# Letting the first expert blocks start before the last scatters, with a third of the expert weights loaded in the last main beat

## The reference

```python
x = x + attention(layernorm(x))               # causal, rotary positions
h = layernorm(x).reshape(4096, 256)
topv, topi = top_k(h @ gate_w.T, 8)           # 8 of 64 experts for each token
rw = softmax(topv)
gu = einsum('nh,eih->nei', h, gu_w)           # 64 gate and 64 up values for each expert
out_e = (silu(gate) * up * W) @ dp_w          # W holds rw at the chosen experts, 0 elsewhere
out = sum over experts of out_e + sigmoid(h @ sg) * shared_ffn(h)
x = x + out
```

## Time and profile before

| what | value |
|---|---|
| runs | 1210.23, 1207.71, 1210.20 us |
| median | 1210.2 us |
| span of the profiled execution | 1382.2 us |
| instructions | 23533 |
| TensorE matmul busy | 1080.5 us (78%) |
| DVE busy | 703.8 us (51%) |
| ACT busy | 647.6 us (47%) |
| POOL busy | 722.5 us (52%) |

### The profile page before, as it was taken

One profiled execution on the slowest core, in us unless ns is written; L12 is line 12 of the kernel. 1 busy time (PEld: TensorE's weight loads), 2 busy tenths in 40 slices (PEclk: granted clock), 3 DMA queues, 4 the chain that ended last, 5 costly groups with the idle time before them and its releaser, 6 DMA issues.

```text
span 1382.2 us, 23533 instructions
## 1 busy us (share of the span) xinstructions
PE 1080.5 (78%) x7305; PEld 833.1 (60%) x7305; DVE 703.8 (51%) x2197; ACT 647.6 (47%) x1586; POOL 722.5 (52%) x953
## 2 busy tenths in 40 slices
PE   3799998888888888889765058887888878787875
PEld 1566666565565656566534047777777767676763
DVE  3476766666666666656525411121245544444447
ACT  2465656555555555655331024444445444444441
POOL 3111225657466564564566735655565565655552
PEclk9699999999999989989877569999999999998996
DMA  2586877212122121122228855555767777776536
GB/s 82 174 288 221 275 256 237 101 48 95 51 84 93 53 90 51 59 102 61 84 93 289 269 172 161 172 169 154 238 233 251 268 268 248 259 243 238 170 138 212
DMA packets 142824, 233.18 MB, mean 169 GB/s; under 512 B 17303, under 2 KB 119910, under 8 KB 137840
## 3 DMA queue, kind: packets, MB, share of 16 engines
q1 hardware_dynamic: 67936, 101.06, 22.7%
q0 software_dynamic: 27600, 69.28, 14.1%
q10 hardware_dynamic: 47168, 61.35, 13.5%
HBM read 107.32 MB, written 132.53 MB: 174 GB/s over the span
## 4 chain that ended last, share of the span: by engine, by line
PE 46%; DVE 16%; another core or an unknown queue 14%; issue 13%; ACT 8%; POOL 1%; DMA 1%; ACTq 0%; SPq 0%; DVEq 0%; POOLq 0%
PE psB L1412 6%; DVE nmax L868 6%; PE psD L1429 5%; PE psv L607 4%; PE ps L511 4%; PE psA L1402 4%; PE ps L558 3%; PE ps L518 3%; PE psp L490 3%; PE psp L504 3%; PE psC L1420 3%; ACT xT L1297 2%; ACT y L1313 2%; PE psq L634 2%
## 5 line engine op out<-in xcount | busy, mean ns | idle before, releaser
L1497 POOL DMA_INDIRECT res_d<-y,dst_i x319 | 320.9, 1006 | 231.9 <-ACT y L1313 117.8
L463 POOL DMA_INDIRECT rows_d<-pay,slot_i x256 | 256.5, 1002 | 75.4 <-issue 73.4
L868 DVE TENSOR_REDUCE nmax<-ps 128x1 f32<-128x512 f32 (+3 forms) x448 | 225.8, 531 | 135.8 <-PE ps L518 93.5
L736 ACT ACTIVATE wgu_s<-ps 128x512 f32<-128x512 f32 x320 | 191.9, 600 | 123.4 <-PE ps L518 91.3
L1216 DVE TENSOR_TENSOR inner<-inner,psB 128x128 f32<-128x128 f32 x160 | 45.8, 286 | 316.8 <-ACT inner L1302 250.5
L1429 PE MATMUL psD<-wdp_s,innerT 128*128 x638 | 174.8, 397 | 21.1 <-ACT innerT L1306 17.6
L1412 PE MATMUL psB<-wgu_s,xT 128*128 x1276 | 179.1, 285 | 1.2 <-ACT xT L1297 0.8
L518 PE MATMUL ps<-mask,ident_b 128*128 128x256 bf16 (+1 forms) x640 | 175.4, 274 | 0.4 <-issue 0.4
L511 PE MATMUL ps<-kT,qT 96*128 96x512 f32 (+3 forms) x512 | 168.3, 391 | 8.1 <-DVE nmax L868 4.8
L558 PE MATMUL ps<-qT,kT 128*128 128x512 f32 (+3 forms) x512 | 165.8, 387 | 4.9 <-ACT wgu_s L736 4.2
L1412 PEld LDWEIGHTS psB<-wgu_s,xT 128*128 128x128 f32 x1276 | 163.9, 201 | 1.8 <-issue 1.2
(11 more groups left out here) (256 smaller groups left out, 1620.0 us busy)
## 6 DMA issues: line engine op xcount, KB each, us to landing
rows_d<-blank ACTq DMA_DIRECT2D x8, 5440.0 KB, 19.3
xg<-rows_d SPq DMA_DIRECT2D x160, 272.0 KB
yk<-res_d SPq DMA_DIRECT2D x28, 1024.0 KB
wgu_s<-wgu_in ACTq DMA_DIRECT2D x8, 1024.0 KB
x_d<-x SPq DMA_DIRECT2D x30, 192.5 KB
xs<-x_d SPq DMA_DIRECT2D x30, 192.5 KB, 2.5
res_d<-y,dst_i POOLq DMA_INDIRECT x319
wgu_s<-x_in SPq DMA_DIRECT2D x32, 128.0 KB, 2.2
```

What stands on the lines that cost most here:

```text
L463: pool.indirect_dma_start(rows_d, bass.IndirectOffsetOnAxis(ap=slot_i[par][:, t, k:k + 1], axis=0), pay[par][:, t, :], None).then_inc(s_sc ...
L736: act.activation(pexp[p % 4][:, s, :], ps2[:, (5 * p + s) % 2, :], ACT.Exp, scale=HEAD_D ** -0.5).then_inc(s_exp, 1)
L868: return dve.tensor_reduce(nmax[u][:, tile, heads[0]:heads[-1] + 1], src, AX.X, ALU.max, negate=True)
L1497: pool.indirect_dma_start(res_d, bass.IndirectOffsetOnAxis(ap=dst_i[:, j % (2 * G):j % (2 * G) + 1], axis=0), y[:, j % Y, :], None, bounds ...
```

## The change

Four things are done.

- SP's wait for the scatters is split. It waits for all of `s_scat[0]`, then, ahead of blocks 0 and 16, for `s_scat[1]` against a value read from SBUF, and ahead of block 32 for all of `s_scat[1]`. The value is computed in the route of the last batch: if some expert's open block lies below block 16 (or 32), it is the full count, otherwise the count without the last batch.
- Two of the eight gate-up parts and two of the four down parts are loaded in the last main beat, at the start of p = 3, 4, 5, 6. The zeroing of the upper partitions beside those two down parts is cut into 16 DVE memsets of 512 columns in the first four slots of p = 4 to 7 of that beat. The other two are zeroed after the attention phase, as before.
- `inner` is zeroed by DVE, not POOL; DVE's first use of `sh` waits for POOL's memset.
- For the value of `needed`, DVE has five short operations more and TensorE one matmul more in the last batch's route.

```diff
+EARLY_BLOCKS = 16
+        EARLY = 2
+        below = cst[0:EXPERTS, C_MASK1:C_MASK1 + EARLY]
+        needed = cst[0:1, C_MASK2:C_MASK2 + EARLY].bitcast(I32)
...
+                        if ending(h, par, 1):
+                            pe.wait_ge(e_open, 3)
+                            pe.matmul(psq[0:EXPERTS, 2:2 + EARLY], ones_f[0:EXPERTS, 0:EXPERTS], below,
+                                      start=True, stop=True)
...
+            EARLY_GU, LATE_GU = (6, 7), (0, 1, 2, 3, 4, 5)
+            EARLY_DOWN, LATE_DOWN = (0, 2), (1, 3)
...
+                    if now and now[0] * 2 + now[1] == BATCH - 1 and s == 0 and now[2] >= 3:
+                        act.wait_ge(s_split_ps, 4 * ALL_TILES)
+                        act.wait_ge(s_s2, (BATCH - 1) * SLOTS)
+                        if now[2] - 3 < len(EARLY_GU):
+                            load_gate_up(EARLY_GU[now[2] - 3])
+                        elif now[2] - 3 - len(EARLY_GU) < len(EARLY_DOWN):
+                            load_down(EARLY_DOWN[now[2] - 3 - len(EARLY_GU)])
...
+                    if h * 2 + par == BATCH - 1 and p >= 4 and s < 4:
+                        n, width = (p - 4) * 4 + s, EXPERTS * D // (8 * TILES)
+                        if n == 0:
+                            dve.wait_ge(s_s2, (BATCH - 1) * SLOTS)
+                        at = EARLY_DOWN[n // 8] * 8 * width + n % 8 * width
+                        last = dve.memset(wdp_s[INNER:P, at:at + width], 0.0)
+                        if n == 15:
+                            last.then_inc(e_padded, 1)
...
+                    if k == 0 and ending(h, par, 1):
+                        dve.wait_ge(s_pool, 12 * b)
+                        dve.tensor_scalar(col[:, 15:16], col[:, 0:1], col[:, 1:2], 2.0 ** 20, ALU.is_ge,
+                                          ALU.mult).then_inc(e_open, 1)
+                        dve.wait_ge(e_open, 1)
+                        dve.scalar_tensor_tensor(out=col[:, 15:16], in0=col[:, 0:1], scalar=col[:, 2:3],
+                                                 in1=col[:, 15:16], op0=ALU.add, op1=ALU.add).then_inc(e_open, 1)
+                        dve.wait_ge(e_open, 2)
+                        dve.tensor_scalar(below, cst[0:EXPERTS, C_BLK + EARLY_BLOCKS:C_BLK + EARLY * EARLY_BLOCKS + 1:
+                                                     EARLY_BLOCKS], col[:, 15:16], None, ALU.is_gt).then_inc(e_open, 1)
...
+                        if ending(h, par, 1):
+                            last_batch = 16 * TILES * TOP
+                            dve.tensor_scalar(below[0:1], psq[0:1, 2:2 + EARLY], 0.5, float(last_batch), ALU.is_gt,
+                                              ALU.mult).then_inc(e_open, 1)
+                            dve.wait_ge(e_open, 4)
+                            dve.tensor_scalar(needed, below[0:1], float(last_batch * (BATCH // 2 - 1)), None,
+                                              ALU.add).then_inc(e_needed, 1)
...
-                for par in range(2):
-                    sp.wait_ge(s_scat[par], 16 * TILES * TOP * BATCH // 2)
+                sp.wait_ge(s_scat[0], 16 * TILES * TOP * BATCH // 2)
+                sp.wait_ge(e_needed, 1)
...
+                    if j % EARLY_BLOCKS == 0 and j // EARLY_BLOCKS < EARLY:
+                        n = j // EARLY_BLOCKS
+                        scattered = sp.value_load(needed[0:1, n:n + 1], min_val=16 * TILES * TOP * (BATCH // 2 - 1),
+                                                  max_val=16 * TILES * TOP * BATCH // 2)
+                        sp.wait_ge(s_scat[1], scattered)
+                    if j == EARLY * EARLY_BLOCKS:
+                        sp.wait_ge(s_scat[1], 16 * TILES * TOP * BATCH // 2)
...
-                dve.memset(wdp_s[INNER:P, :], 0.0).then_inc(e_wdp_zero, 1)
+                for part in LATE_DOWN:
+                    last = dve.memset(wdp_s[INNER:P, part * EXPERTS * D // TILES:(part + 1) * EXPERTS * D // TILES], 0.0)
+                last.then_inc(e_padded, 1)
+                for t in range(TILES):
+                    dve.wait_ge(s_x2out[t], 16 * (2 * BATCH - 1) if t < 2 else 16)
+                dve.memset(inner[:], 0.0).then_inc(e_padded, 1)
...
+                    if tile == 0:
+                        dve.wait_ge(e_zero, 1)
...
-                act.wait_ge(e_zero, 2)
+                act.wait_ge(e_padded, 3)
...
-                pe.wait_ge(e_wdp_zero, 1)
+                pe.wait_ge(e_padded, 2)
...
-                pool.memset(inner[:], 0.0).then_inc(e_zero, 1)
```

More of the change, by code:

```diff
@@ L81, in build @@
         e_wdp = sem("down_weights_in")
-        e_wdp_zero = sem("down_weights_padded")
+        e_padded = sem("down_weights_and_inner_padded")
+        e_open, e_needed = sem("open_blocks"), sem("scatters_needed")
         waits_met = sem("waits_met")
@@ L737, in exps, with load_gate_up, load_down @@
                                    scale=HEAD_D ** -0.5).then_inc(s_exp, 1)
-                def main(now, one, two, s):
+                def load_gate_up(part):
+                    width = EXPERTS * KC * GU // (2 * TILES)
+                    cut = slice(part * width, (part + 1) * width)
+                    act.dma_start(wgu_s[:, cut], wgu[:, cut]).then_inc(e_w, 16)
+                def load_down(part):
+                    width = EXPERTS * D // TILES
+                    cut = slice(part * width, (part + 1) * width)
+                    act.dma_start(wdp_s[0:INNER, cut], wdp[:, cut]).then_inc(e_wdp, 16)
+                def main(now, one, two, s):
+                    if now and now[0] * 2 + now[1] == BATCH - 1 and s == 0 and now[2] >= 3:
[5 more added lines that the diff above has]
+                            load_down(EARLY_DOWN[now[2] - 3 - len(EARLY_GU)])
                     if now and isinstance(now[0], int):
@@ L773, in post @@
                         act.wait_ge(s_s2, BATCH * SLOTS)
[L774 to L781, removed]
+                        part = (t - 2) * 6 + k
+                        if part < len(LATE_GU):
+                            load_gate_up(LATE_GU[part])
+                        elif part - len(LATE_GU) < len(LATE_DOWN):
+                            load_down(LATE_DOWN[part - len(LATE_GU)])
                     if k == 1:
```

## The result

| what | before | after |
|---|---|---|
| median of the runs | 1209.45 us (4 runs, 1207.71 to 1210.23) | 1196.03 us (4 runs, 1193.35 to 1196.32) |
| ratio of after to before | | 0.9879, 95% interval 0.9863 to 0.9896 |

The change makes the kernel 14.6 us faster ((1 - 0.9879) x 1209.45; by the interval 12.6 to 16.6). The ratio is the recorded one with its interval and not the quotient of the two medians, which is 0.9889 and would give 13.4 us. The prediction was 15.3 us.

What follows compares the result with a forecast made beforehand. Without the unknown pieces POOL was taken as slightly slower than TensorE, the two near even later. Gain 19.6 less cost 4.3 (4 + 1.5 - 1.2) is 15.3 us: 1210.2 to 1194.9 us, range 1184 to 1206.

Steps and rivals of the forecast that it cites:

- the unknown pieces: Chain time in the first profile put down to nothing known, 14%; taken as mostly the profiler's own.
- The rival in which TensorE and ACT pace: Expert phase: TensorE's whole ten-block lead counts, 24 to 28 us less 4.3, about 1188 us; chance 0.13.
- a span near 1359: Profiled execution after the change: at 1.69 us a block, 27.9 us gained less 4.3, from 1382.2.
- step 1: SP's gate: loads may start once batch 6 lands, at 764; reading a value 1.5 us, priced at nothing.
- step 2: Weights at the handover: a third less to load late, 17.7 us earlier; TensorE starts at about 780, not 809.
- step 4: POOL at the handover: 14.1 us saved plus 3.7 of early starvation, 17.8; with TensorE's lead 21.4; middle taken, 19.6.
- step 5: The 16 memsets in the last main beat: cost 4 us, half hidden, bounds 0 and 8.8.
- The other bound, a bare 8.8: Memsets in the last main beat not hidden; as a rival, with 2 us of route, about 1203 us; chance 0.16.
- steps 6 and 7: Last batch: longer route costs 1.5 us on the path; ACT's four DMA issues leaving its post save 1.2 us.
- slower-side rival: Expert phase: TensorE's clock stays low after its pause; gain gone at some 63 us, 1235 us at 50 blocks; chance 0.04.

Runs made afterwards that it cites:

- before_again: The kernel before, unchanged, profiled once more (also written "before, again"): 1209.27 us, profiled span 1207.5 us.
- pool_slower: late_zeros with 39 memsets of 768 columns on POOL, one before every eighth block: 1213.51 us, ratio to the kernel before 1.0038.
- gate_only: The changed kernel with all twelve weight parts and all zeroing back behind the attention phase, SP's split wait kept: 1191.78 us, ratio 0.9869.
- late_zeros: The changed kernel without the 16 memsets, all 16,384 columns zeroed after the attention phase, early weights kept: 1191.6 us, ratio 0.9848.
- zeros_thrice: The changed kernel with each of the 16 memsets done three times, each waiting for the one before: 1210.33 us, ratio 1.0001.
- weights_only: The changed kernel with SP again waiting for all scatters before its first load: 1210.92 us, ratio 1.001.
- no_pool_wait: late_zeros without POOL's wait for its last rows_d scatter and its zeroing of `sh`, which DVE does at first use: 1189.88 us, ratio 0.984.
- eight_early: late_zeros with gates at blocks 4 and 8, so 8 blocks and not 32 may go ahead of the last scatters: 1197.62 us, ratio 0.9903.

## Why the prediction was right

**What paces.** The argument was that the unknown pieces of the profile are its own and that POOL paces behind the handover. before_again shows the first. The second is shown by POOL's idle time in after, by ACT's 94.8 us for room in `y`, and by pool_slower, where a delay of 23.8 us put into POOL's queue showed as 21.8. The rival in which TensorE and ACT pace falls with it. The forecast of a span near 1359 was wrong: it took over from one execution a stretching that the next one didn't have.

**The gate opens (step 1).** Shown: SP's first load is at 718.55, 5.2 us behind the end of batch 6's last scatter where 3.3 were forecast (762.24 to 764 + 1.5), and POOL has 28 of batch 7's scatters still to issue. The count of the reference's choices held.

```profile
718.55 81.56 SPq L1217 DMA_DIRECT2D xg<-rows_d  x35
```

**TensorE's start (step 2).** Forecast 15.5 us behind the first scatter of batch 7, held by the weights; measured 7.6 us (721.25 - 713.66), held by the loads: the last weight part is issued at 689.83 and lands 25.8 us later, at 715.6, before SP's first load. Wrong by 8 us, on the safe side, and worth nothing, since POOL was busy for 32 us more. For the same reason the weights part, which the step counted as 17.7 us, is worth nothing: gate_only shows it.

**POOL at the handover and behind it (step 4).** Forecast 14.1 + 3.7 = 17.8; measured 13.98 + 3.18 = 17.16. The step then went up to 19.6, halfway to the 21.4 that TensorE's lead would give if TensorE paced the later blocks. That is the part that failed: POOL has no waits behind block 95 either, after or in before, again, so the lead is worth nothing. The gain was 2.4 too high.

**The 16 memsets (step 5).** The mechanism is right (partly hidden in DVE's gaps), the size is not: forecast 4, measured 1.0. I had taken as cover only the 5.7 us ahead of the reductions that wait for TensorE, read from the stretched execution, whose row puts another 12.3 us ahead of the same reductions down to other causes. In before, again DVE waits 11.4 us for TensorE's scores in that part of the beat, and after 5.0: the cover was twice what I had read, and the memsets used 6.4 us of it. By the runs alone 4 could not be excluded (3.7 in late_zeros). The other bound, a bare 8.8, nearly comes true for each further round: 16.5/2 = 8.3 us in zeros_thrice.

**Route and ACT's issues (steps 6 and 7).** Forecast +1.5 and -1.2; measured 0 and 0 within what can be read: 86.67 us before, again, 86.95 after, and 86.66 in weights_only, from batch 6's `slot_i` to the last rows_d scatter. The step had the route of batch 7 on the path because POOL idled 2.26 us for it. In before, again POOL has no such gap: it goes from 708.93 to 710.19 in its usual step. After, batch 7's slots are ready while POOL is still in batch 6's scatters:

```profile
708.33 0.18 DVE L333 TENSOR_SCALAR slot_i<-slot_f 128x32 int32<-128x32 f32 x1
```

POOL's last scatter of batch 6 starts at 712.39, 3.9 us behind its end. So POOL's own queue sets the start of batch 7's scatters, and a longer route is hidden. The 2.26 us belonged to the stretched execution.

**The sum.** Forecast 19.6 - 4.3 = 15.3; by terms measured 17.2 - 1.0 = 16.2, the trace has 16.0, the runs 14.6. The gain was too high by 2.4 and the cost by 3.3, and they cancelled in part: that the total is so close (0.7 us from the runs) is luck, two errors in gain and cost that offset each other. Either error alone would have left the time inside the range of 1184 to 1206.

**The clock.** TensorE's idle time was the slower-side rival. It came as described: TensorE stops for 12.66 us.

```profile
763.29 2.04 PE L1498 MATMUL psD<-wdp_s,innerT 128*128 x4 [12.66 <-ACT innerT L1375]
```

It resumes at 1.2 GHz, that is at 0.50 in 755 to 765 (the windows above), shows 0.68 in 765 to 770 and 1.00 from 770, the 2.4 GHz level. Low clock thus ends less than 7 us after the restart, and ten blocks lie ready, so POOL never sees it; the rival needed 63 us. (It took 2.35 us a block at that level; half of its 4.74 is 2.37, which changes nothing.) The Trainium skill (TensorE: Matmul & The Clock Gate, HAM oscillation) describes such a swing; the trace agrees, with this one dip (1.00, 0.50, 1.00) behind the handover, and it had no price here.

## What to carry to other kernels

Ask which queue paces behind a handover and work out a gain only from the waits of that queue: here POOL's wait was worth its 14 + 3 us to the end, while a third of the weights loaded early was worth nothing, nor was it that the first blocks lay ready 24 us before POOL took them. Price an added piece against the waits of its engine in that stretch, read from an execution that is not stretched, and remember that this cover is used up: the first 16 memsets cost a tenth of their length, the next 32 four fifths. Where a profile's span is far from the time of the runs, profile the same kernel again before you read waits and gaps in it, and compare executions from a marker, not from their start.

## What the hardware showed that I had not expected

- **How late a POOL scatter lands when weights are loading.** SP's first load waits for the last scatter of batch 6 to land. It follows that scatter's end by 5.2 us after (713.35 to 718.55), and by 2.7, 4.0, 4.4 and 2.7 us in late_zeros, no_pool_wait, eight_early and pool_slower; about 1 us of each is SP's own reading of the value. In gate_only, where all twelve weight parts load late, it follows by 15.9 us (706.44 to 722.35), at a DMA share of 1.01 in 706 to 722, and that SP waits there for the scatters is in its waits (us in all, times, longest):

```profile
SPq L1202 <- DMA rows_d<-pay,slot_i: 7.4, 1, 7.4
```

  In before, again, where the weights are late as well, the landing itself comes 18.1 us behind the end of that scatter, against 14.9 in gate_only and 4.0 after. POOL went on issuing every 1.27 us all the while. The cause inside the DMA engines was not tried; here it was hidden.
- **A memset's row is shorter than the memset.** The two late memsets after, of 4096 columns:

```profile
710.16 3.47 DVE L1248 MEMSET wdp_s<- 64x4096 f32 x1 [0.91 <-DMA x_d<-oT]
714.43 3.47 DVE L1248 MEMSET wdp_s<- 64x4096 f32 x1 [0.80 <-DMA x_d<-oT]
```

  From start to start it is 4.27 us, 1.04 ns a column, against 0.85 by the row. The Trainium skill (VectorE: DVE Perf Modes, Zero memsets can be issued as uint32) has one cycle an element, 1.04 ns at the 0.96 GHz of its Specifications; by the spacing the trace agrees, by the row it doesn't. The idle time that nothing explains ahead of a memset grows with its length: 0.16 us at 512 columns, 0.80 at 4096, and 3.47 at 16,384 in before, again. (The releaser named at 0.80 is not it: the same 0.80 stands in gate_only between late memsets with no releaser.)
- **A memset on POOL among scatters costs less than its row**: 0.61 us for a row of 0.78, since the gap behind it is 0.16 us and not 0.30 and it starts before the scatter's row has quite ended.
- **One profiled execution can be stretched**: 1382.2 us of span against 1207.5 for the same kernel, with idle pieces on ACT, DVE and TensorE that nothing explains, while POOL's own spacing stays at its 1.27 and 1.29 us.
